# Attention denominators kept in 16 rows, inverted once per batch, and an earlier place for phi and the key sums

## The reference

```python
x = x + 0.5 * ffn(layernorm(x), Wg, Wu, Wd)      # 8 experts, hidden 128, FFN 512; the sum over all experts
x = x + attention(layernorm(x), Wq, Wk, Wv, Wo, bo)
x = x + 0.5 * ffn(layernorm(x), Wg, Wu, Wd)

def expert_step(acc, w):                         # scanned over the 8 experts
    h = silu(x @ wg) * (x @ wu)
    return acc + h @ wd
```

```python
S = S + phi_k[:, None] * v[None, :]              # per head, 8 x 8
z = z + phi_k                                    # per head, 8
out = (phi_q @ S) / (sum(phi_q * z) + 1e-5)      # one denominator per head and token
```

## Time and profile before

| what | value |
|---|---|
| median of 3 runs | 2146.64 us (2146.49 to 2147.45) |
| profiled execution | 2146.52 us, its span 2144.8 us |
| granted clock of TensorE, mean | 0.998 |
| PE busy | 2102.3 us, 98% |
| DVE busy | 1836.3 us, 86% |
| ACT busy | 1421.4 us, 66% |
| POOL busy | 406.5 us, 19% |
| DMA | 92.42 MB, 15.4% of 16 engines |

### The profile page before, as it was taken

The page is one execution under the profiler, slowest core; times in us unless marked ns, Lnnn a source line. Parts: engine busy times, 40 slices in busy tenths (PEclk is TensorE's granted clock), DMA queues, the critical chain, the costliest instruction groups (busy, mean ns, idle before and its releaser), DMA issues.

```text
span 2144.8 us, 29776 instructions
## 1 busy us (share of the span) xinstructions
PE 2102.3 (98%) x9856; PEld 971.7 (45%) x9856; DVE 1836.3 (86%) x3086; ACT 1421.4 (66%) x2481; POOL 406.5 (19%) x331
## 2 busy tenths in 40 slices
PE   6999999999999999999999999999999999999999
PEld 2444444444444444444444444444444444444444
DVE  8877798878988898899788978898889898988776
ACT  5767766776677666666766676567666766666665
POOL 0001022302221132122212312122112122230000
PEclk9999999999999999999999999999999999999999
DMA  7000121004010410023003020311031112210000
GB/s 202 1 1 1 54 74 50 1 11 118 11 45 8 106 57 14 16 68 94 11 13 97 16 63 11 99 40 30 1 103 45 45 34 52 64 45 6 6 4 7
DMA packets 44842, 92.42 MB, mean 43 GB/s; under 512 B 3088, under 2 KB 24208, under 8 KB 44688
## 3 DMA queue, kind: packets, MB, share of 16 engines
q1 hardware_dynamic: 44688, 90.52, 15.4%
HBM read 77.92 MB, written 12.58 MB: 42 GB/s over the span
## 4 chain that ended last, share of the span: by engine, by line
PE 87%; DVE 6%; ACT 3%; issue 3%; DMA 0%; SPq 0%; ACTq 0%; DVEq 0%
PE bank L429 9%; PE bank L441 9%; PE bank L442 9%; PE bank L443 9%; PE bank L420 9%; PE bank L418 9%; PE bank L419 9%; PE bank L430 9%; PE bank L431 9%; DVE bank L710 2%; DVE h_lo L715 2%; ACT silu_sb L539 1%; DVE arena L821 1%; PE bank L504 1%; PE bank L473 1%
## 5 line engine op out<-in xcount | busy, mean ns | idle before, releaser
L539 ACT ACTIVATE silu_sb<-bank,scal 128x512 f32<-128x512 f32 x1024 | 703.7, 687 | 653.0 <-PE bank L420 649.1
L710 DVE SCALAR_TENSOR_TENSOR bank<-silu_sb,scal,bank 128x512 f32<-128x512 f32 x1024 | 769.1, 751 | 283.6 <-ACT silu_sb L539 279.6
L715 DVE TENSOR_TENSOR h_lo<-bank,h_hi 128x512 f16<-128x512 f32 x1024 | 693.4, 677 | 0.1
L545 ACT ACTIVATE h_hi<-bank 128x512 f16<-128x512 f32 x1024 | 604.4, 590 | 10.2 <-DVE bank L710 9.7
L429 PE MATMUL bank<-xn_hi,wu_hi 128*128 128x512 f16 x1024 | 389.4, 380 | 18.1 <-DVE h_lo L715 14.3
L418 PE MATMUL bank<-xn_hi,wg_hi 128*128 128x512 f16 x1024 | 389.1, 380 | 3.0 <-DVE wg_lo L704 3.0
L419 PE MATMUL bank<-xn_lo,wg_hi 128*128 128x512 f16 x1024 | 389.1, 380 | 0.0
L420 PE MATMUL bank<-xn_hi,wg_lo 128*128 128x512 f16 x1024 | 388.9, 380 | 0.0
L430 PE MATMUL bank<-xn_lo,wu_hi 128*128 128x512 f16 x1024 | 388.6, 380 | 0.0
L431 PE MATMUL bank<-xn_hi,wu_lo 128*128 128x512 f16 x1024 | 388.6, 380 | 0.0
L443 PE MATMUL bank<-h_lo,wd_hi 128*128 128x512 f16 x1024 | 388.1, 379 | 0.0
(11 more groups left out here) (117 smaller groups left out, 1328.8 us busy)
## 6 DMA issues: line engine op xcount, KB each, us to landing
arena<-rep_scratch SPq DMA_DIRECT2D x128, 512.0 KB, 6.4
rep_scratch<-arena SPq DMA_DIRECT2D x16, 512.0 KB, 2.8
x_tok<-in_L_attn_x SPq DMA_DIRECT2D x16, 256.0 KB, 5.4
out<-x_tok SPq DMA_DIRECT2D x16, 256.0 KB, 2.4
arena<-in_L_ffn_Wg SPq DMA_DIRECT2D x4, 512.0 KB, 6.2
arena<-in_L_ffn_Wu SPq DMA_DIRECT2D x4, 512.0 KB, 9.3
arena<-in_L_ffn_Wd SPq DMA_DIRECT2D x4, 512.0 KB, 10.0
wq_raw<-in_L_attn_Wq SPq DMA_DIRECT2D x1, 64.0 KB, 4.9
```

The source lines that it names most:

```text
L539: act.activation(silu_sb[:, n % 3, :], gate_ps[n % NG][:, :], ACT.Silu, scale=unscale[G]).then_inc(sem("silu"), 1)
L545: act.activation(h_hi[:, n % NH, :], up_ps[n % NUP][:, :], ACT.Copy).then_inc(sem("h_hi"), 1)
L710: dve.scalar_tensor_tensor(up_ps[n % NUP][:, :], silu_sb[:, n % 3, :], h_scale, up_ps[n % NUP][:, :], ALU.mult, ALU.mult).then_inc(sem("h" ...
L715: dve.tensor_tensor(h_lo[:, n % NH, :], up_ps[n % NUP][:, :], h_hi[:, n % NH, :], ALU.subtract).then_inc(sem("h_lo"), 1)
```

## The change

`head_ones` becomes 128 x 16, so that `den` gives one row per head (16 partitions), and `den_evac` writes 16 rows of `rden`. These go to DRAM and come back as `den_all`, 128 partitions x 128 tokens, with eight partitions a head. One `recip` per batch inverts them, in place of eight. They go to DRAM again and are brought back into all of `rden`, each head's row repeated to eight partitions. `att_out` waits for that last transfer. In the planner `phi`, `z_scan` and `q_z` move from `att_rounds` into `att_head`, so they get their steps before the rounds of the batch ahead; `den` may not come before the end of the batch ahead (as before), and rounds not before the last `num_add` of the batch ahead. `PACE` goes from 11 to 10 and `ATT_STEP` from 100 to 98.

```diff
--- before.py
+++ after.py
@@ -25,8 +25,8 @@
 
 LAG = 4
 
-PACE = 11
-ATT_STEP = 100
+PACE = 10
+ATT_STEP = 98
 NORM_LEAD = 18
 
 SPARE = 680
@@ -167,11 +167,7 @@
             t += 1
         act_at[t].append(("exp", b))
         load.update({t + k: SPARE for k in range(1, 4)})
-        return t
-
-    def att_rounds(b, t, before):
-
-
+        exp_at.append(t)
         t += 4
         for a in blocks_of(b):
             t = vector(t, "phi_k", a, T + 64, True)
@@ -179,46 +175,55 @@
         for a in blocks_of(b):
             t = vector(t, "phi_q", a, T + 64, True)
         sp_at[t].append(("store_q", b))
-        stored = t
-        begin = u = t + 2
+        begin = t
         for a in blocks_of(b):
             t = vector(t, "z_scan", a, 2 * T + 64, True)
             z = gpsimd(t, "q_z", a, 1)
-            recip = take(max(z + 2, before), "den", a) + 3
-            act_at[recip - 2].append(("den_evac", a))
+        return begin, z
+
+    def att_rounds(b, stored, t, before, rounds):
+
+
+        begin = v = max(stored + 2, rounds)
+        for a in blocks_of(b):
+            u = take(max(t, before), "den", a)
+            act_at[u + 1].append(("den_evac", a))
+
+
+        sp_at[u + 2].append(("den_store", b))
+        sp_at[u + 4].append(("den_load", b))
+        recip = vector(u + 7, "recip", b, 7 * P)
+        sp_at[recip].append(("rden_store", b))
+        sp_at[recip + 2].append(("rden_load", b))
+        recip += 6
         for d in range(D):
             r = b * D + d
-            u = max(u, begin + PACE * d)
 
             n = 2 + (d > 1)
-            u = gpsimd(u, "k_v", r, n)
+            v = gpsimd(max(v, begin + PACE * d), "k_v", r, n)
             if d > 1:
-                pool_at[u - n].insert(-1, ("num_add", r - 1))
-            sp_at[max(u - 6, stored)].append(("k_rep", r))
-            sp_at[max(u - 6, stored)].append(("q_rep", r))
-            t = u
+                pool_at[v - n].insert(-1, ("num_add", r - 1))
+            sp_at[max(v - 6, stored)].append(("k_rep", r))
+            sp_at[max(v - 6, stored)].append(("q_rep", r))
             for j in range(BB):
-                t = vector(t, "kv_scan", BB * r + j, 2 * T + 64, True)
+                v = vector(v, "kv_scan", BB * r + j, 2 * T + 64, True)
             for j in range(BB):
-                t = vector(t, "q_state", BB * r + j, T + 64, True)
-            u = t
-        u = gpsimd(u, "num_add", r, 2)
-        for i in range(D):
-            recip = vector(recip, "recip", b * D + i, 7 * P)
+                v = vector(v, "q_state", BB * r + j, T + 64, True)
+        u = gpsimd(v, "num_add", r, 2)
         t = max(u + 1, recip)
         for a in blocks_of(b):
             t = vector(t, "att_out", a, T + 64, True)
         for a in blocks_of(b):
             t = take(t + 1, "wo", a, "att_resid")
         assert t + 2 <= NC * seg_of[2, b * BB] - NORM_LEAD
-        return t
-
-    exp_at, end = [], 0
+        return t, u
+
+    exp_at, heads, ends = [], [], (0, 0)
     for b in range(B + 1):
         if b < B:
-            exp_at.append(att_head(b, NC * BB + LAG + 5 + ATT_STEP * b))
+            heads.append(att_head(b, NC * BB + LAG + 5 + ATT_STEP * b))
         if b:
-            end = att_rounds(b - 1, exp_at[b - 1], end)
+            ends = att_rounds(b - 1, *heads[b - 1], *ends)
     FIRST, LAST = -1, NU + LAG + 8
 
 
@@ -280,13 +285,14 @@
         var_eps, rstd = sb("var_eps", [P, 4, TT]), sb("rstd", [P, 4, TT])
         shift = sb("shift", [P, 4, TT])
         minus_half = sb("minus_half", [P, TT])
-        ident, head_ones, ones = sb("ident", [P, P]), sb("head_ones", [P, P]), sb("ones", [P, P])
+        ident, head_ones, ones = sb("ident", [P, P]), sb("head_ones", [P, HEADS]), sb("ones", [P, P])
         max_diag = sb("max_diag", [P, P])
         watt_raw = [sb(f"w{w}_raw", [P, P]) for w in "qkvo"]
         watt_t = [sb(f"w{w}_T", [P, P]) for w in "qkvo"]
         watt_hi = [sb(f"w{w}_hi", [P, P], F16) for w in "qkv"]
         watt_lo = [sb(f"w{w}_lo", [P, P], F16) for w in "qkv"]
         bo_all = sb("bo_all", [P, P])
+        den_all = sb("den_all", [P, HEADS * L // P])
         warm = sb("warm", [P, TT])
         amax_part = sb("amax_part", [P, 3, NP])
 
@@ -304,6 +310,7 @@
         NG, NUP = 3, 3
         gate_ps, up_ps, down_ps, misc_ps = psum[0:3], psum[3:6], psum[6], psum[7]
         rep_d = nc.dram_tensor("rep_scratch", (B, 2, P, L), F32, kind="Internal").ap()
+        den_d = nc.dram_tensor("den_scratch", (B, 2, HEADS, L), F32, kind="Internal").ap()
 
         sems = {}
 
@@ -379,6 +386,23 @@
                             sp.wait_ge(sem("q_state"), BB * (i - NR + 1))
                         src = rep_d[b, 1, :, :].rearrange("(h d) t -> h d t", d=D)[:, d:d + 1, :]
                         sp.dma_start(ring("q_rep", i), src.to_broadcast([HEADS, D, L])).then_inc(sem(f"q_rep{i % NR}"), 16)
+                    elif kind == "den_store":
+                        sp.wait_ge(sem("den_evac"), BB * (i + 1))
+                        sp.dma_start(den_d[i, 0, :, :], rden[0:HEADS, :]).then_inc(sem("den_store"), 16)
+                    elif kind == "den_load":
+                        sp.wait_ge(sem("den_store"), 16 * (i + 1))
+                        if i:
+                            sp.wait_ge(sem("rden_store"), 16 * i)
+                        sp.dma_start(den_all[:, :], den_d[i, 0, :, :].rearrange("h (c t) -> (h c) t", c=D)
+                                     ).then_inc(sem("den_load"), 16)
+                    elif kind == "rden_store":
+                        sp.wait_ge(sem("recip"), i + 1)
+                        sp.dma_start(den_d[i, 1, :, :].rearrange("h (c t) -> (h c) t", c=D), den_all[:, :]
+                                     ).then_inc(sem("rden_store"), 16)
+                    elif kind == "rden_load":
+                        sp.wait_ge(sem("rden_store"), 16 * (i + 1))
+                        src = den_d[i, 1, :, :].rearrange("h (a t) -> h a t", a=1)
+                        sp.dma_start(rden, src.to_broadcast([HEADS, D, L])).then_inc(sem("rden_load"), 16)
                     elif kind == "out":
                         blk = segs[i][1]
                         sp.wait_ge(sem("resid"), i + 1)
@@ -494,7 +518,7 @@
                     elif kind == "den":
                         pe.wait_ge(sem("q_z"), i + 1)
                         take_turn(kind, i)
-                        pe.matmul(misc_ps[:, :], head_ones[:, :], ql[:, cols(i % BB)], start=True, stop=True
+                        pe.matmul(misc_ps[0:HEADS, :], head_ones[:, :], ql[:, cols(i % BB)], start=True, stop=True
                                   ).then_inc(sem("den"), 1)
                     elif kind == "wo":
                         pe.wait_ge(sem("att_out"), i + 1)
@@ -625,7 +649,7 @@
                         act.wait_ge(sem("den"), i + 1)
                         if b:
                             act.wait_ge(sem("att_out"), BB * b)
-                        act.activation(rden[:, cols(j)], misc_ps[:, :], ACT.Copy, bias=ATT_EPS
+                        act.activation(rden[0:HEADS, cols(j)], misc_ps[0:HEADS, :], ACT.Copy, bias=ATT_EPS
                                        ).then_inc(sem("den_evac"), 1)
                     elif kind == "watt_copy":
                         act.wait_ge(sem("watt_T"), i + 1)
@@ -832,13 +856,12 @@
                         dve.tensor_tensor(state if d else num[:, cols(j)], ring("q_rep", r)[:, cols(j)], state, ALU.mult
                                           ).then_inc(sem("q_state"), 1)
                     elif kind == "recip":
-                        b, d = divmod(i, D)
-                        dve.wait_ge(sem("den_evac"), BB * b + d // TT + 1)
-                        dve.reciprocal(rden[:, cols(d, P)], rden[:, cols(d, P)]).then_inc(sem("recip"), 1)
+                        dve.wait_ge(sem("den_load"), 16 * (i + 1))
+                        dve.reciprocal(den_all[:, :], den_all[:, :]).then_inc(sem("recip"), 1)
                     elif kind == "att_out":
                         b, j = divmod(i, BB)
                         dve.wait_ge(sem("num_add"), added(b * D + D - 1) - BB + j + 1)
-                        dve.wait_ge(sem("recip"), D * b + TT * (j + 1))
+                        dve.wait_ge(sem("rden_load"), 16 * (b + 1))
                         dve.tensor_tensor(num[:, cols(j)], num[:, cols(j)], rden[:, cols(j)], ALU.mult
                                           ).then_inc(sem("att_out"), 1)
                     elif kind == "att_resid":
@@ -881,13 +904,12 @@
             pool.affine_select(out=ident[:, :], in_=ident[:, :], compare_op=ALU.not_equal, fill=1.0,
                                base=0, pattern=[[-1, P]], channel_multiplier=1)
 
-            by_head = head_ones[:, :].rearrange("p (h d) -> p h d", d=D)
             pool.wait_ge(sem("pool_one"), 1)
-            pool.affine_select(out=by_head, in_=by_head, compare_op=ALU.is_ge, fill=0.0,
```

(7 more changed lines are left out.)

## The result

The changed kernel takes 2141.46 us (median of 11 runs, 2140.88 to 2141.8) against 2146.2 us of the kernel before (11 runs on the same chips, 2145.3 to 2147.45): a ratio of 0.9978 with a 95% interval of 0.9968 to 0.9987. That is 4.7 us faster, where 6.5 were forecast. That is 0.2% of the time, small but outside the interval. The experiments show that the sum came out near for the wrong reasons, that is by luck.

A forecast was written before the change was run, and what follows sets the result against it. TensorE's stalls, 25 us caused by VectorE's extra work, were taken as all there was to win; 6.5 us gained from fewer reciprocals and 0 from the rest gave 2140 us, range 2132 to 2151.

The forecast's parts named there:

- What bounds the kernel: TensorE, busy 98%: time moves only by its stalls, nearly all before the first `up` matmul, 25 us to win.
- The split of the 25 us into 6, 6 and 13: TensorE's stalls divided into table loads at exponentials, VectorE work lengthened beside POOL, and plain VectorE congestion.
- (b): Scans and products on VectorE lengthened by meeting POOL instructions: some 6 us of TensorE stall.
- (a): Stalls around the exponentials, where ScalarE loads tables and VectorE waits: about 6 us, untouched by the change.
- (c): Plain congestion, VectorE behind by several fillers in a row: the remaining 13 us of TensorE stall.
- Fewer reciprocals: 56 fewer on VectorE, 52.9 us less work there; congestion stalls of TensorE shrink, 6.5 us gained.
- The plan: Moved `phi`, `z_scan`, `q_z` and tighter rounds: same work elsewhere, planned load no higher; 0, with 6 us either way.
- 16 columns of weights: Denominator matmuls: weight load lies under the matmul ahead, so 0; outside values 0 and 3 us less.
- The round trip: Denominators via DRAM: 9.2 to 12.8 us from second `den`, 13.6 us available; no VectorE wait, at most 8 x 2 us.
- The rival with `den_load`: VectorE waits for the denominators' late DRAM load: 22 to 48 us less 6.5, 2162 to 2188 us; chance 9%.
- More collisions: `phi` and `z_scan` meet POOL's work more often, eleven more meetings at 1.1 us: 2152 us; chance 7%.
- What I said would show it: About 8 reciprocals without idle ahead, first `up` matmul's `h_lo` wait under 55.5 us, VectorE about 85% busy, table-load stalls unchanged.

The follow-up runs named there:

- w128: The changed kernel with `head_ones` 128 columns wide instead of 16, 16 rows still evicted, all else as changed: 2138.22 us, ratio 0.9961.
- oldplan_newden: The changed kernel with `head_ones` 128 columns wide and the planner of the kernel before: 2146.13 us, ratio 0.9998.
- dummies_last: `w128` with seven more 128x128 reciprocals per batch, results unused, planned after everything else so nothing moves: 2139.04 us, ratio 0.9968.
- late_load: `w128` with the reciprocal planned 3 instead of 7 steps after the second `den`, and its DRAM load done four times in sequence: 2200.21 us, ratio 1.0248.

## Why the prediction was right, and where it wasn't

- *Sum:* 6.5 us forecast for the profiled run, 5.2 measured in the span. That the two are near is luck. The path from before to after, in this order of steps, is 0.4 (denominators) + 6.6 (constants) + 1.3 (order, not separated from nothing) - 3.2 (narrow weights) = 5.1 us (from the 2146.6 us that the kernel before took beside `w128`), where the forecast had 6.5 for the first and 0 for the others.
- *What bounds the kernel:* right. TensorE's instructions kept their number, and what moved were its stalls: 5.8 of the 8.0 us at the first `up` matmul, the rest at other matmuls, as at L447 above. That some 25 us were all there was to win wasn't put to the test, as no kernel won more than 8.3.
- *The split of the 25 us into 6, 6 and 13:* by the table's count (b), the meetings, was near (6.7 us). (a), the exponentials, is 12.7 us when the stalls just ahead of one are counted too, and what is left for (c), the congestion, is 7.8 us and not 13. So the 6.5 us forecast would have been nearly all of (c).
- *Fewer reciprocals, 6.5 us:* this step failed, though the 56 reciprocals did leave VectorE, which was busy 40.8 us less in `oldplan_newden`. It assumed that stall follows VectorE's average load, with TensorE's unbroken run at 71% as its other end. That end was a stretch without attention, so it differed in more than load. The second support, 7.0 us of stall with a reciprocal in the 9 us ahead of it, was nearness and no cause: with those reciprocals gone the wait was the same in as many places. They had been put in room that no one else had taken. As time on VectorE they are worth 0.4 us (old plan) to 0.8 us (`dummies_last`). In the new plan the new denominators as a whole are worth 3.9 us, and the other 3.1 came with the items that moved.
- *The plan, taken as 0 with 6 us either way:* the mis-sized term. It carried 4.4 us by itself and 7.9 with the new denominators, more than the bound of 6, which counted only the meetings and not the place of the exponentials. I had named both as kinds (a) and (b) of the stall and then treated (a) as untouched.
- *16 columns of weights, 0 or up to 3 us less:* the sign was wrong. I bounded it by the length of the weight load and held its cover for given; the narrower load lost its cover, and it cost 3.2 us.
- *The round trip, no wait:* right, with more room than I gave it. The second `den` of batch 0 starts at 275.60 and its load has landed at 282.80, 7.2 us later where I had 9.2 to 12.8; the reciprocal starts at 290.46. A 64 KB transfer took 1.5 to 1.9 us. `k_rep` behind `rden_store` did no harm either: POOL's wait for these loads fell from 58.0 to 7.4 us.
- *The rival with `den_load`:* it didn't come, but its price, 22 to 48 us, was too low. It is 62 us, since hardly any of the wait is absorbed and the clock falls too.
- *More collisions:* the opposite came. Eleven scans and products were long before, five after. The prediction has the later of two instructions pay. In rows 6 and at 1005.90 it was the scan that paid, though it is recorded 0.02 us ahead of POOL's addition; so these rows bear out the size of the price and not who pays it.
- *What I said would show it:* about 8 reciprocals, L453's wait under 55.5 us, VectorE near 85%: the first two came true and the third nearly (85.9%), and none of them could tell a load that matters from a plan that matters. Only the parts taken singly did. The sign that I gave for a failed step from load to stall, VectorE emptier and the stall no smaller, is what `oldplan_newden` then showed.

## What to carry to other kernels

On an engine that fills another's gaps, average load says little: find out which crowds and which meetings end in a stall, since work taken out of leftover room gave nothing back here. A change that comes with new schedule constants has to be split into the edit and the constants before a gain is put down to the edit. And before an operand on the bounding engine is made narrower, look whether the overlap it has is kept.

## What the runs showed of the hardware

- Float32 matmuls whose weights have 16 or 64 columns had their weight load exposed, and the load of the matmul behind them too (1.27 and 1.31 us for a stretch that takes 1.07 us with 128 columns). Whether it is the columns of the weights or the rows written, and whether the same holds for float16, wasn't tried.
- A scan on VectorE (1.22 us) that starts within 0.02 us of a POOL addition of two SBUF tiles takes 2.37 us, and the POOL instruction keeps its 1.27 us, although the scan's record starts first. This was so before and after (rows 6 and the timeline at 1005.90).
- After 4.7 us without a matmul (`late_load`) TensorE's granted clock was at the lower level for 3.4 us, and so for 3.4 to 10.2 us after each of the other seven gaps. From 40 us to the last matmuls, stalls up to 1.6 us in the other kernels left it at 1.00. Ahead of 40 us, with gaps of 2.6 to 4.1 us, it was lower for 6.8 us in some kernels (the one before) and never in others (the one after).
